# Graph network with routed experts on one core: the residual rows and the scatters of the second experts go straight to the output tensor

## The reference, cut to what matters

```python
top_p, top_idx = jax.lax.top_k(probs, TOP_K)                  # TOP_K = 2 of 8 experts
weights = top_p / top_p.sum(axis=-1, keepdims=True)
h = jax.nn.gelu(jnp.einsum('end,edh->enh', xe, W1) + b1[:, None, :], approximate=False)
y = jnp.einsum('enh,ehd->end', h, W2) + b2[:, None, :]
...
out = (weights[:, :, None] * sel).sum(axis=1)                 # sel: the rows of y of a node's two experts
...
x = x + _L1_ffn_ref(_layernorm(x, axis=-1)[None], ...)[0]     # what the kernel returns
```

## Time and profile before

| | |
|---|---|
| time, median of 3 runs | 2167.11 us (2167.04 to 2168.02) |
| profiled execution, its own time | 2173.45 us |
| span of the profiled execution, first to last instruction | 2171.7 us |
| TensorE busy | 1798.3 us (83%) |
| GpSimd busy | 1138.5 us (52%) |
| granted TensorE clock, mean | 0.891 of full speed |

### The profile page before, as it was taken

The page is one execution under the profiler, slowest core; times in us unless marked ns, Lnnn a source line. Parts: engine busy times, 40 slices in busy tenths (PEclk is TensorE's granted clock), DMA queues, the critical chain, the costliest instruction groups (busy, mean ns, idle before and its releaser), DMA issues. The chain is left out here.

```text
span 2171.7 us, 40952 instructions
## 1 busy us (share of the span) xinstructions
PE 1798.3 (83%) x12824; PEld 1513.5 (70%) x12825; DVE 1296.6 (60%) x2708; ACT 928.2 (43%) x1837; POOL 1138.5 (52%) x1156
## 2 busy tenths in 40 slices
PE   5737988888766999699529999999688699999996
PEld 4526766666645877566328888788577599999995
DVE  7238977777768542346478889899549622222221
ACT  5426765555544244356342222222245533433441
POOL 2677777777750300146567777677530134544442
PEclk9958987787877899799769999999887799999998
DMA  3597665555556453467568766666641667777775
GB/s 94 152 208 199 172 165 152 159 156 154 158 125 154 96 151 104 121 196 217 172 206 253 248 222 213 198 231 227 216 124 48 198 194 195 192 190 200 192 193 144
DMA packets 201875, 379.40 MB, mean 175 GB/s; under 512 B 43573, under 2 KB 137706, under 8 KB 201551
## 3 DMA queue, kind: packets, MB, share of 16 engines
q1 hardware_dynamic: 136743, 223.25, 34.3%
q0 software_dynamic: 64176, 152.51, 26.9%
q10 hardware_dynamic: 840, 2.16, 0.3%
HBM read 273.60 MB, written 107.64 MB: 176 GB/s over the span
## 5 line engine op out<-in xcount | busy, mean ns | idle before, releaser
L833 POOL DMA_INDIRECT qr<-q_rows,src_t x415 | 396.3, 955 | 126.5 <-issue 125.9
L2379 PE MATMUL psP<-f_part,onehot 125*128 125x256 bf16 x3600 | 410.6, 275 | 27.4 <-DVE onehot L2405 27.3
L2359 POOL DMA_INDIRECT fr<-pair_rows,dst_i x372 | 355.0, 954 | 127.9 <-issue 109.4
L2379 PEld LDWEIGHTS psP<-f_part,onehot 125*128 125x128 bf16 x3600 | 354.0, 99 | 75.5 <-DVE onehot L2405 32.1
L931 PE MATMUL psK<-kp,oh_k 126*128 x1680 | 280.3, 325 | 85.7 <-DVE qr L1045 57.7
L931 PEld LDWEIGHTS psK<-kp,oh_k 126*128 126x128 bf16 x1680 | 187.5, 113 | 161.9 <-issue 92.5
L1960 ACT ACTIVATE m1hT<-m1psH,m1par 128x128 f32<-128x128 f32 x448 | 127.7, 368 | 255.1 <-PE m1psH L1980 255.1
L2417 DVE SCALAR_TENSOR_TENSOR psA<-psA,same,fr 128x256 f32<-128x256 f32 x420 | 206.3, 491 | 37.1 <-DVE psA L2417 14.7
L1980 PEld LDWEIGHTS m1psH<-m1xT,n_rows 128*128 128x128 f32 x1792 | 210.3, 193 | 5.5 <-DMA n_rows<-in_L_ffn_W_dram 2.7
L1980 PE MATMUL m1psH<-m1xT,n_rows 128*128 128x128 f32 x1792 | 210.8, 276 | 2.5 <-DMA n_rows<-in_L_ffn_W_dram 2.5
L2003 PE MATMUL m1psY<-w_all,m1hT 128*128 x896 | 203.7, 381 | 0.0
(11 more groups left out here) (509 smaller groups left out, 2825.3 us busy)
## 6 DMA issues: line engine op xcount, KB each, us to landing
n_rows<-in_L_ffn_W_dram SPq DMA_DIRECT2D x56, 1024.0 KB, 6.3
run_rows<-acc SPq DMA_DIRECT2D x84, 640.0 KB
loc<-locals_ SPq DMA_DIRECT2D x85, 157.5 KB
ea<-in_edge_attr_dram SPq DMA_DIRECT2D x84, 140.0 KB
w_first<-in_L_ffn_Wd_dram SPq DMA_DIRECT2D x8, 1024.0 KB, 11.8
w_all<-in_L_ffn_W_dram SPq DMA_DIRECT2D x8, 1024.0 KB, 9.9
m1b<-in_L_ffn_b_dram SPq DMA_DIRECT2D x56, 128.0 KB, 2.9
qr<-q_rows,src_t POOLq DMA_INDIRECT x420
```

The costliest lines, as they stand in the source:

```text
L833: nc.gpsimd.indirect_dma_start(out=qr[:, n % GQ, u, :], out_offset=None, in_=q_rows, in_offset=bass.IndirectOffsetOnAxis(ap=src_t[:, n, u: ...
L2359: nc.gpsimd.indirect_dma_start(out=fr[:, n % GI, u, :], out_offset=None, in_=f_rows, in_offset=bass.IndirectOffsetOnAxis(ap=f_at[:, n * G ...
L2379: last = nc.tensor.matmul(psP[:, k % 2, 0:D], onehot[:, k % 2, t, :], f_part[:, c, t, :], start=(t == 0 and c == 0), stop=(t == T - 1 and ...
```

## The change

The tensor `sum1` is gone. SyncE stores the residual rows to `out`, and the 56 scatters add to `out`. Since `out` has no spare rows, the scatters get a bound: indices above N_NODES − 1 are left out, without an error. The fill of the spare rows at L1325 goes, with it the 16 in GpSimd's wait, and so does the last block with its barrier and its three copies.

```diff
-        sum1 = dram("sum1", [N_NODES + 2 * S, D])
...
             @block.sync
             def _(sp):
-                sp.dma_start(sum1[N_NODES:N_NODES + 2 * S], x[0:2 * S]).then_inc(s_base[1], 16)
                 sp.wait_ge(s_root3, 1)
...
                         nc.gpsimd.indirect_dma_start(out=total, out_offset=bass.IndirectOffsetOnAxis(ap=to_i[:, b:b + 1], axis=0),
-                                                     in_=yr[b % 2][:], in_offset=None, compute_op=ALU.add).then_inc(s_yst[b % 2], 16)
+                                                     in_=yr[b % 2][:], in_offset=None, bounds_check=N_NODES - 1, oob_is_err=False,
+                                                     compute_op=ALU.add).then_inc(s_yst[b % 2], 16)
...
-                    pool.wait_ge(s_base, 32 * NG + 16)
+                    pool.wait_ge(s_base, 32 * NG)
...
                     for a, b in HALVES:
-                        sp.dma_start(rows_of_tiles(sum1[0:N_NODES])[a:b, i * G:(i + 1) * G, :], x_sb[a:b, i * G:(i + 1) * G, :])\
+                        sp.dma_start(rows_of_tiles(out)[a:b, i * G:(i + 1) * G, :], x_sb[a:b, i * G:(i + 1) * G, :])\
                           .then_inc(s_base[1], 16)
...
-        experts("m1", NB1, tok1, s_tok[1], sum1, s_base[1], L1_ffn_W1, L1_ffn_W2, L1_ffn_b2, True)
-
-        s_out = sem("out_stored")
-        with ExitStack() as st:
-            block = st.enter_context(nc.Block(no_gpsimd_drain=True))
-            PARTS11 = ((0, 1560), (1560, 3120))
-
-            @block.scalar
-            def _(act):
-                act.dma_start(out[PARTS11[0][0]:PARTS11[0][1]].rearrange("(n r) d -> n (r d)", r=5),
-                              sum1[PARTS11[0][0]:PARTS11[0][1]].rearrange("(n r) d -> n (r d)", r=5)).then_inc(s_out, 16)
-
-            @block.sync
-            def _(sp):
-                sp.dma_start(out[PARTS11[1][0]:PARTS11[1][1]].rearrange("(n r) d -> n (r d)", r=5),
-                             sum1[PARTS11[1][0]:PARTS11[1][1]].rearrange("(n r) d -> n (r d)", r=5)).then_inc(s_out, 16)
-                sp.dma_start(out[PARTS11[1][1]:N_NODES], sum1[PARTS11[1][1]:N_NODES]).then_inc(s_out, 16)
-                sp.wait_ge(s_out, 48)
+        experts("m1", NB1, tok1, s_tok[1], out, s_base[1], L1_ffn_W1, L1_ffn_W2, L1_ffn_b2, True)
```

## The result

The changed kernel takes 2144.98 us (median of 4 executions, 2141.47 to 2153.04) against 2167.07 us (4 executions, 2165.0 to 2168.02): ratio 0.9917 [0.9895, 0.9939]. The medians lie 22.1 us apart; the ratio, which is not that of the two medians, stands for 18 us (13 to 23). Three later comparisons of the same two kernels gave 0.9929 [0.9898, 0.9959], 0.994 [0.9915, 0.9965] and 0.9931 [0.9914, 0.9949]; the forecast, 2154.1 / 2167.11 = 0.994, lies in all three. The experiments with e1 to e4 and e13 to e18 ran on chips on which the stages ahead of the second experts take some 410 us longer (the kernel before takes 2571 to 2579 us there); with them only ratios, stretches and tails are compared. One execution of e4 took 2967.49 us at a granted clock of 0.617 and is left out of its ratio.

What follows compares the result with a forecast made beforehand. TensorE was taken to bound the second experts' stretch, with a copy hidden behind nothing at the end. Copy and empty scatters −13.76, late gathers +0.8, sum −13.0: 2167.11 − 13.0 = 2154.1 us; 8-in-10 range 2151.0 to 2159.5.

Steps and rivals of the forecast that it cites:

- The copy and its barrier: Program's end: with nothing behind the last scatter's landing, the span ends 12.45 us sooner.
- Empty scatters: Last two scatters: without rows they land in 3.1 us, not 3.8, GpSimd's work 1.3; 1.3 us saved.
- The price of the bound: Each scatter: register move 0.03 us plus GpSimd's index comparison 0.07, together 0.1 us.
- +0.8 for the 8 late gathers: Second experts: 0.1 us more per scatter is paid where TensorE already waits for the gather, 8 × 0.1 us.
- Elsewhere it stays inside the margin: Second experts' other blocks: a later gather costs nothing, its margin being 0.5 us, or up to 3.2.
- The third rival: Empty scatters land under 2.8 us and lighter traffic removes half of 7.3 us late gathers: 2149.0 us; chance 0.11.
- The second: Rival: the bound doubles GpSimd's scatter work (+1.62 us) and the row gather becomes the bound: 2185 us; chance 0.06.
- The fourth: Rival: out takes additions more slowly than sum1; one us more per landing gives 2156; chance 0.28 shared with The first.
- The first: Rival: left-out rows save nothing, only the copy counts: 2155.5 us, up to 2163.8; chance 0.28 shared with The fourth.

Runs made afterwards that it cites:

- e1: The changed kernel run again unaltered, on a chip with slower earlier stages: 2561.97 us, 0.9929 of the kernel before.
- e4: The kernel before, its scatters given a bound that leaves out no row; copy and target as before: 2575.09 us, ratio 0.998.
- e13: The changed kernel unaltered, one more profiled execution on a chip with slower earlier stages: 2556.86 us.
- e18: The changed kernel with the bound in a register filled once, profiled on a chip with slower earlier stages: 2557.6 us.
- e7: The kernel before with rows beyond the nodes left out of the scatters; sum1, fill and copy kept: 2163.69 us, ratio 0.9998.
- e3: The kernel before with only the copy of 5 rows left, 3120 output rows not written: 2572.81 us, ratio 0.998.
- e5: The changed kernel unaltered, as the measure for others on one chip: 2152.03 us, 0.994 of the kernel before.
- e6: The changed kernel with the bound in a register filled once ahead of the blocks: 2149.46 us, 0.9932 of the kernel before.
- e10: The changed kernel unaltered, run again on another chip: 2149.86 us, 0.9931 of the kernel before.
- e9: The changed kernel with a useless GpSimd fill, and a wait for it, ahead of each scatter: 2149.94 us, 0.994 of the kernel before.
- e11: The kernel before with only the gather of rows moved to four blocks ahead, before the scatter: 2156.07 us, ratio 0.9959.
- e14: The changed kernel unaltered, a second profiled execution on a chip with slower earlier stages: 2558.59 us.
- e12: The kernel before unaltered, one more profiled execution: stretch of the second experts 424.3 us; no execution time given.

## Why the prediction was wrong

**The copy and its barrier: right.** −12.45 was forecast. e7 leaves the same rows out and keeps the copy, and its tail is 15.6 us against 3.2, so 12.4 us are the copy's block alone. e3 shows that most of it is the copy's data. From TensorE's last matmul to the end the span shrank by 13.95 us, against −13.76 for this and the empty scatters together.

**Empty scatters: right in sign, one part wrong.** Forecast 3.1 us to the landing with 1.3 of GpSimd's work; it is 2.75 with 1.56 to 1.59. GpSimd's work does not shrink; what follows it does (1.2 us, forecast 1.8). The rule of the Trainium skill (DMA: Bandwidth & Descriptors, Anatomy of one DMA) would have made it 3.5, an estimate, with only the bytes saved. The measurement decides against that here. That −13.76 came so near is partly luck: the two landings are 0.35 and 0.37 us shorter than forecast, while the scatter of block 54 starts 0.82 us behind VectorE's step where 0.30 was reckoned, and block 55 starts 0.88 us after the landing where 0.80 was.

**The price of the bound: the mis-sized term.** "0.1 us per scatter" is 0.55 (e5 against e6). The move is 0.03 us as SyncE's is; but the wait for VectorE sits on it, and 0.76 us come behind it where 0.28 came behind the wait before. GpSimd's comparison of the indices costs nothing that shows (1626 against 1624 ns). What followed in the sum, +0.8 for the 8 late gathers, is not what happened: the five traces with the move and few waits have a median stretch of 425.5 us, the five without it 425.6. TensorE's matmuls wait more often (11 to 17 times, not 7 to 9) and about as long in all (5.1 to 9.1 us, against 6.8 to 8.7). In e4 and e5 the longer waits of the weight loads go with 430 us; e10's 423.5 shows no such cost.

**The step that failed** is "Elsewhere it stays inside the margin", and with it the range. A scatter 0.55 us later is not held by that margin: it comes from 2.3 us ahead of W1's request to 1.8, at block 3 to 1.0, and in 7 of 12 traces 12 or 50 scatters then waited for one another, which the sum has no term for. In the two with 50 the stretch is 413.4 and 414.7 us.

I took the stretch of the second experts as one number, and the three runs of before, within 1 us of each other, as what a time of this kernel is good for. Neither holds. The three comparisons at this speed gave −22.1, −11.0 and −14.8 us between the medians. On chips of the speed of the first comparison the changed kernel took 2136.53 to 2156.44 us in 19 executions (median 2149.76), the kernel before 2154.55 to 2176.82 in 38 (median 2164.47): 14.7 us between the medians, where −13.0 was forecast, and a spread that a range of 8.5 us cannot hold. So of the 9.1 us by which the first comparison's difference went beyond the forecast's, 7.4 come from its few executions, as far as medians tell (the kernel before stood 2.6 us above the median of all, the changed one 4.8 below), and 1.7 from the sum.

Two sources of spread are shown: the first gather comes at 1719.4 to 1728.1 us whatever the kernel, and in the old order of the gathers, e9 apart, the stretch is 413 to 415 us in an execution in which 50 scatters wait, 421 to 431 in the others. The late gathers (11 us of stretch, e11) are what vanishes then. The third rival allowed half of 7.3 us for that, by lighter traffic. Lighter traffic alone is not it: e13 and e14 are the same kernel with the same rows left out, and 11 us of stretch lie between them with 50 waits and with 2.

**Rivals.** The second (GpSimd's work doubled) is out: 1626 against 1624 ns. The fourth (the output takes additions more slowly) is out: full scatters land in a median of 3.8 to 3.9 us to either tensor (before and e12; e5 and e6), and late landings come to both (e7 and the first trace of the changed kernel). The first is out too, empty scatters land sooner.

**What stays open.** Of the four executions of the first comparison only the one of 2153.04 was traced, with 12 waits and a stretch of 424.2. That those of 2141 to 2142 us had 50 is likely by size (2153 − 11 = 2142) and not shown: no execution of the changed kernel under 2152 us was profiled on such a chip. Twelve traces with a move ahead of each scatter had 1, 2, 3, 12 or 50 waits, seven without it 0 or 1, so the later start seems to be needed for the waiting order, and what then decides between 2, 12 and 50 was not found. Nor was it found why block 3's scatter starts 0.7 us later than block 2's. Whether the rows left out are needed too is open: all traces with 12 or 50 waits have them left out, and e4, the one trace with the move and all rows, had 2.

## What to carry to other kernels

A tail in which no engine works is a gain whose size could be read off one trace here (12.45 us forecast, 12.4 measured). When a DMA gets a register operand, look for which instruction the wait lands on, and fill the register once, ahead of the loop. Before a range is drawn, the spread over executions has to be priced like a term. Where a stream stands at small margins (here a gather that TensorE waits for 8 times in 56), the order should be mended first: gathering one block further ahead gave −8.6 us on the kernel before, and with the change and one register 2140.2 us, 0.9896 [0.987, 0.9923], the best version.

## What was unexpected of the hardware

- An indirect DMA from GpSimd starts 0.76 us behind the end of a register move that held the wait (0.83 us behind VectorE's step, e5), and 0.28 us behind VectorE's step when it holds the wait itself (e6).
- An indirect accumulating scatter of which all 128 rows are beyond the bound still takes GpSimd 1.56 to 1.59 us and lands 2.75 us after its start, where one with all its rows takes 1.62 and lands in 3.8 to 3.9.
- The same scatter lands in 3.9 us when W1's transfer of 1 MB is requested 1.8 us behind its start, and in 6.3 us (median in e7) when that request comes mostly 0.5 to 0.9 us behind it; the gather behind them lands in 5.1 us in the first case (e5) and in 3.7 in the second.
